# A two-layer decoder: context turned by the host's layout, first batch's parts made a stage earlier, and a fused mask and maximum

## The reference, cut to what matters

```python
x = _layernorm(x + _L0_attn_ref(x, ...))                        # 16 heads, 4 key heads, window + front
x = _layernorm(x + _L0_xattn_ref(x, ctx_2048, mask_BxS2_bk0))   # one head of width 512
x = _layernorm(x + _L0_ffn_ref(x, ...))
x = _layernorm(x + _L1_attn_ref(x, ...))                        # 16 heads of width 128, causal
x = _layernorm(x + _L1_xattn_ref(x, ctx_2048, ctx_2048))
x = _layernorm(x + _L1_ffn_ref(x, ...))

# _L0_xattn_ref
scores = jnp.einsum('bsd,bmd->bsm', hidden_states, memory_tokens) * scale
scores = jnp.where(memory_mask[:, None, :], scores, neg_inf)
attn = jax.nn.softmax(scores, axis=-1)
readout = jnp.einsum('bsm,bmd->bsd', attn, memory_tokens)
out = jnp.where(valid_b[:, None, None], readout, jnp.zeros_like(readout))
# _L1_attn_ref
scores = jnp.where(causal, scores, IGNORE); attn = softmax(scores)
```

## Time and profile before

| | |
|---|---|
| median of 3 runs | 2108.53 us (2105.29 to 2111.03) |
| profiled execution, whole | 2107.33 us |
| its span, first to last instruction | 2105.6 us |
| busy: PE, DVE, ACT, POOL | 1917.6, 1338.3, 1085.0, 638.0 us |
| mean granted clock | 0.954 |

### The profile page before, as it was taken

How to read it: one execution, slowest core, us unless ns; L and a number is a source line. 1 busy time by engine, 2 the same in 40 slices (tenths; PEclk the granted TensorE clock), 3 DMA queues, 4 the chain that set the end, 5 groups by cost and what they waited for, 6 DMA issues and landing times. The chain is left out here.

```text
span 2105.6 us, 35999 instructions
## 1 busy us (share of the span) xinstructions
PE 1917.6 (91%) x12824; PEld 1185.5 (56%) x12824; DVE 1338.3 (64%) x2579; ACT 1085.0 (52%) x2135; POOL 638.0 (30%) x558
## 2 busy tenths in 40 slices
PE   7999769989999999989999999998888876999998
PEld 4666534468887788844545454453555552455553
DVE  6777665465565755676658476687899846454333
ACT  4777543243333433356536264473799973344333
POOL 4666311123333333212101011010576740133220
PEclk9999979989999999999999999998799968999999
DMA  5000023111110111205011100003500004566433
GB/s 187 27 27 2 1 109 118 46 52 50 50 50 26 50 50 41 67 22 145 21 40 41 41 20 1 1 1 76 133 3 2 2 27 149 181 181 180 122 70 96
DMA packets 103178, 131.96 MB, mean 63 GB/s; under 512 B 8264, under 2 KB 61640, under 8 KB 103008
## 3 DMA queue, kind: packets, MB, share of 16 engines
q1 hardware_dynamic: 96304, 114.20, 17.6%
q0 software_dynamic: 6720, 15.73, 3.8%
HBM read 103.83 MB, written 22.87 MB: 60 GB/s over the span
## 5 line engine op out<-in xcount | busy, mean ns | idle before, releaser
L1113 POOL TENSOR_TENSOR wl<-stage,wh 128x512 fp32r<-128x512 f32 x80 | 116.0, 1475 | 271.9 <-DVE wh L1108 271.9
L2890 POOL TENSOR_TENSOR PTl<-P,PTh 128x512 f16<-128x512 f32 (+2 forms) x160 | 148.8, 937 | 121.1 <-ACT PTh L3014 118.4
L1699 POOL TENSOR_TENSOR Zl<-z,Zh 128x512 f16<-128x512 f32 x32 | 51.1, 1597 | 428.0 <-ACT Zh L1862 428.0
L3013 ACT ACTIVATE P<-PS 128x512 f32<-128x512 f32 (+3 forms) x256 | 143.7, 561 | 43.2 <-PE PS L2958 42.6
L77 PE MATMUL PS<-XTh,wh 128*128 128x512 f16 x416 | 159.2, 383 | 7.4 <-DVE tri L2024 5.4
L78 PE MATMUL PS<-XTl,wh 128*128 128x512 f16 x416 | 158.9, 382 | 0.0
L79 PE MATMUL PS<-XTh,wl 128*128 128x512 f16 x416 | 158.7, 381 | 0.0
L3014 ACT ACTIVATE PTh<-PS 128x512 f16<-128x512 f32 (+3 forms) x256 | 145.4, 568 | 0.0
L3030 DVE TENSOR_REDUCE M<-PS 128x1 f32<-128x640 f32 (+3 forms) x128 | 127.0, 1012 | 4.4 <-PE PS L2942 4.4
L1351 ACT ACTIVATE h<-PS,bup 128x512 f32<-128x512 f32 x64 | 44.1, 689 | 147.0 <-PE PS L79 146.3
L2958 PE MATMUL PS<-QS,KS 98*128 98x512 f16 (+3 forms) x256 | 99.6, 390 | 18.6 <-ACT PTh L3014 14.2
(11 more groups left out here) (381 smaller groups left out, 5893.5 us busy)
## 6 DMA issues: line engine op xcount, KB each, us to landing
stage<-in_ffn_W SPq DMA_DIRECT2D x18, 1024.0 KB, 5.2
stage<-in_ffn_Wg SPq DMA_DIRECT2D x9, 1024.0 KB, 5.2
stage<-in_ffn_Wup SPq DMA_DIRECT2D x16, 512.0 KB, 3.9
stage<-in_ffn_Wdn SPq DMA_DIRECT2D x16, 512.0 KB, 3.7
wq<-in_attn_wq SPq DMA_DIRECT2D x4, 1024.0 KB, 6.6
C<-in_ctx SPq DMA_DIRECT2D x8, 512.0 KB, 8.3
stage<-in_ffn_Wsw SPq DMA_DIRECT2D x16, 256.0 KB, 3.4
stage<-in_attn_WV SPq DMA_DIRECT2D x16, 256.0 KB, 4.5
```

Source lines behind the costliest of these rows:

```text
L1113: self.c.nc.gpsimd.tensor_tensor(self.piece(self.low[q], ch), self.piece(self.stage, ch), plain(self.piece(self.high[q], ch)), ALU.subtrac ...
L1699: nc.gpsimd.tensor_tensor(Zl[:, hh, to], z32[:, uu % 2, :], Zh[:, hh, to], ALU.subtract).then_inc(z_lo, 1)
L2890: ops.tensor_tensor(PTl[:, (CT * n + kt) % RING, cols], P32[:, (CT * n + kt) % SLOTS, cols], PTh[:, (CT * n + kt) % RING, cols], ALU.subtr ...
L3013: nc.scalar.activation(P32[:, i % SLOTS, cols], c.PS[:, 4 + i % 2, cols], ACT.Exp, scale=SC)
```

## The change

Three parts. (1) The host also passes the context turned (`ctxT`, a layout of the same numbers), and `turn_context` is gone. A new object `Cross0Front` holds the first batch's turned parts, two stages for pieces of 256 context rows, the mask, the mask row and the ones; its memory is that of the second cross attention's front, not yet in use. The first batch's four pieces are loaded and split during the first self-attention (units 6, 7, 14, 15), its mask row is made after unit 8; `wh` and `wl` there go from four slots to two. (2) In the first cross attention, ACT and DVE split four plain context tiles ahead of the first maximum and four in round 0, pieces 4 to 7 (the second batch) in rounds 0 and 1, and context tiles 8 to 15 in rounds 2 and 3; `Vh` holds one batch; the stores move. (3) In the second self-attention the mask product goes, and DVE's reduction and scaling become one `tensor_tensor_reduce` as in the first; PE's bank is free at that maximum; ACT's exponential reads `Pr` in place. `causal` is a new 128 x 512 constant. The bias comes first on DVE, PE waits for no constant, and DVE's four groups are all written out.

```diff
 # phase_attn1, SP
+            sp.dma_start(causal[:], c.inp["c_causal"]).then_inc(causal_in, 16)
 # PE, scores
-                need(pe, exp_done, QT * u + qt - 1)
+                need(pe, max_done, QT * u + qt - 1)
                 products(pe, out, (Qh[:, q, 0, tok], Ql[:, q, 0, tok]),
-                         (Qh[:, q, 1, 0:w], Ql[:, q, 1, 0:w]), stop=False)
-                pe.matmul(c.PS[:, 2 + qt % 2, w - P:w], c.identb[:], tri[:], start=False, stop=True,
-                          skip_group_check=True).then_inc(s_done, 1)
+                         (Qh[:, q, 1, 0:w], Ql[:, q, 1, 0:w])).then_inc(s_done, 1)
-            pe.wait_ge(const_done, 2)
             body(0)
 # ACT, exp
-                act.wait_ge(bias_done, QT * u + qt + 1)
-                need(act, t_done, QT * (u - 1) + qt + 1)
-                nc.scalar.activation(Pr[:, qt, 0:w], c.PS[:, 2 + qt % 2, 0:w], ACT.Exp, bias=nbias[:, i:i + 1],
-                                     scale=SC, accum_out=rsum[:, i:i + 1]).then_inc(exp_done, 1)
+                act.wait_ge(max_done, QT * u + qt + 1)
+                nc.scalar.activation(Pr[:, qt, 0:w], Pr[:, qt, 0:w], ACT.Exp, bias=nbias[:, i:i + 1],
+                                     scale=-1.0, accum_out=rsum[:, i:i + 1]).then_inc(exp_done, 1)
-            act.wait_ge(const_done, 3)
+            act.wait_ge(bias_ready, 1)
 # DVE, maximum
-                nc.vector.tensor_reduce(nmax[:, i:i + 1], c.PS[:, 2 + qt % 2, 0:(qt + 1) * P], AX.X, ALU.max,
-                                        negate=True).then_inc(max_done, 1)
-                dve.wait_ge(max_done, QT * u + qt + 1)
-                nc.vector.tensor_scalar(nbias[:, i:i + 1], nmax[:, i:i + 1], SC, None, ALU.mult).then_inc(bias_done, 1)
+                need(dve, t_done, QT * (u - 1) + qt + 1)
+                if isinstance(u, int) and u == 0 and qt == 2:
+                    dve.wait_ge(shifted, NT)
+                w = (qt + 1) * P
+                nc.vector.tensor_tensor_reduce(out=Pr[:, qt, 0:w], in0=c.PS[:, 2 + qt % 2, 0:w], in1=causal[:, S - w:S],
+                                               scale=-SC, scalar=FAR, op0=ALU.add, op1=ALU.min,
+                                               accum_out=nbias[:, i:i + 1]).then_inc(max_done, 1)
 # DVE, start of the stage
+            dve.wait_ge(bias_in, 16)
+            nc.vector.tensor_scalar(bq[:], bq[:], XS, None, ALU.mult).then_inc(bias_ready, 1)
             dve.wait_ge(front.const_in, 48)
             (casts of triT and tri)
+            dve.wait_ge(const_done, 2)
+            dve.wait_ge(causal_in, 16)
+            for g in range(NG):
+                body(g, g < NG - 1)

+class Cross0Front:
+    PIECES = 4
+    def load(self, sp, i):
+        b, n = divmod(i, self.PIECES)
+        need(sp, self.ct_lo, i - 1)
+        src = self.c.inp["ctxT"][b][:, n * self.W:(n + 1) * self.W].rearrange("(k p) s -> p k s", p=P)
+        sp.dma_start(self.stage[i % 2][:], src).then_inc(self.piece_in[i % 2], 16)
+    def split_hi(self, act, i):
+        act.wait_ge(self.piece_in[i % 2], 16 * (i // 2 + 1))
+        self.c.nc.scalar.activation(self.part(self.high, i), self.stage[i % 2][:], ACT.Copy, scale=XS).then_inc(self.ct_hi, 1)
+    def split_lo(self, dve, i):
+        dve.wait_ge(self.ct_hi, i + 1)
+        self.c.nc.vector.scalar_tensor_tensor(out=self.part(self.low, i), in0=self.stage[i % 2][:], scalar=XS,
+                                              in1=self.part(self.high, i), op0=ALU.mult, op1=ALU.subtract).then_inc(self.ct_lo, 1)
+    def mask_row(self, dve): ...

 # phase_attn0:  AHEAD = [U - 2, U - 1, 2 * U - 2, 2 * U - 1], U = 8
+            after.load_mask(sp)
             for g in range(1, KVH):
+                for i in (2 * g - 2, 2 * g - 1) if g < 3 else ():
+                    after.load(sp, i)
                 load(g)
+                if u in AHEAD:
+                    after.split_hi(act, AHEAD.index(u))        # ACT, end of unit u
+                if u in AHEAD:
+                    after.split_lo(dve, AHEAD.index(u))        # DVE, end of unit u
+                if u == U:
+                    after.mask_row(dve)
+                need(dve, a_done, (REP + 1) * B * (g - 1))     # DVE weights: wh[:, g % 2], wl[:, g % 2]

 # phase_cross0
+        def split_at(t):
+            pieces = [PIECES + 2 * t, PIECES + 2 * t + 1] if t < PIECES // 2 else []
+            first = CT + 4 * (t - PIECES // 2)
+            return pieces, [i for i in range(first, first + 4) if CT <= i < NC]
 # SP
+            for i in range(CT // 2):
+                load(i)
+            front.load(sp, PIECES)
+            front.load(sp, PIECES + 1)
+            for i in range(CT // 2, NC // 2):
+                load(i)
+            front.load(sp, PIECES + 2)
+            front.load(sp, PIECES + 3)
+            store_turned(0)
+            store_values(0)
+            store_turned(1)
             sp.wait_ge(c_lo, NC)
             weights.load(sp, 0, 0)
+            store_values(1)
 # PE: the calls of turn_context and the waits on its tiles go; scores wait for ct_lo, PIECES * (b + 1)
 # ACT: for t in range(4): context_high(t), then in round t
                 exponential of tile t
+                for i in range(4, CT) if t == 0 else ():
+                    context_high(i)
                 high part of the turned weights
+                for i in pieces:
+                    front.split_hi(act, i)
+                for i in tiles:
+                    context_high(i)
 # DVE: for t in range(4): context_low(t), then maximum(0), and in round t
                 maximum(t + 1)
+                for i in range(4, CT) if t == 0 else ():
+                    context_low(i)
                 ...
+                for i in pieces:
+                    front.split_lo(dve, i)
+                for i in tiles:
+                    context_low(i)
```

More of the change, by code:

```diff
@@ L1654, in phase_attn1 @@
         bq = sb("bq", [P, 3, H], F32)
-        tri = cross.tri
+        causal = sb("causal", [P, S], F32)
         Qh = sb("Qh", [P, 2, 2, S], F16)
@@ L2027, in _, with __init__, load_mask, part @@
-            body(0, True)
-            with dve.Fori(1, NG - 1) as g:
-                body(g, True)
-            body(NG - 1, False)
-            norm.late(norm.dve_step, dve)
-def phase_attn0(c, **end):
+            nc.vector.tensor_copy(cross.tri[:], front.tri32[:]).then_inc(const_done, 1)
+            dve.wait_ge(const_done, 2)
+            dve.wait_ge(causal_in, 16)
+            for g in range(NG):
+                body(g, g < NG - 1)
+            norm.late(norm.dve_step, dve)
+class Cross0Front:
+    PIECES = 4
+    W = S2 // PIECES
+    def __init__(self, c, ctx):
+        self.c = c
+        names = [("CTh", [P, KD, S2], F16), ("CTl", [P, KD, S2], F16), ("stage0", [P, KD, self.W], F32), ("stage1", [P, KD, self.W], F32),
+                 ("m32", [P, B, S2 // 4], I32), ("mrow", [1, B, S2], BF16), ("ones", [1, P], BF16)]
+        size = sum(int(np.prod(shape[1:])) * (2 if dt in (F16, BF16) else 4) for _, shape, dt in names)
+        CTh, CTl, *self.stage, self.m32, self.mrow, self.ones = Region(c, c.nc.sbuf_usable_end // 32 * 32 - size, size).place(names)
+        self.high, self.low = [CTh], [CTl]
+        sem = lambda name: ctx.enter_context(c.nc.semaphore(f"cross0_{name}"))
+        self.piece_in, self.m_in = [sem(f"piece{q}_in") for q in range(2)], sem("m_in")
+        self.ct_hi, self.ct_lo, self.m_done = sem("ct_hi"), sem("ct_lo"), sem("m_done")
+    def load(self, sp, i):
[3 more added lines that the diff above has]
+        sp.dma_start(self.stage[i % 2][:], src).then_inc(self.piece_in[i % 2], 16)
+    def load_mask(self, sp):
+        sp.dma_start(self.m32[:], self.c.inp["mask"].partition_broadcast(P)).then_inc(self.m_in, 16)
+    def part(self, parts, i):
+        b, n = divmod(i, self.PIECES)
+        return parts[b][:, :, n * self.W:(n + 1) * self.W]
+    def split_hi(self, act, i):
[5 more added lines that the diff above has]
+                                              in1=self.part(self.high, i), op0=ALU.mult, op1=ALU.subtract).then_inc(self.ct_lo, 1)
+    def mask_row(self, dve):
+        dve.wait_ge(self.m_in, 16)
+        self.c.nc.vector.tensor_scalar(self.mrow[:], self.m32[:].bitcast(U8)[0:1], 1.0, -NEG, ALU.subtract, ALU.mult).then_inc(self.m_done, 1)
+        self.c.nc.vector.memset(self.ones[:], 1.0).then_inc(self.m_done, 1)
@@ L2046, in phase_attn0 @@
+def phase_attn0(c, after, **end):
     nc = c.nc
@@ L2570, in _, with phase_cross0 @@
                 norm.low(dve, t)
-def phase_cross0(c, weights, **end):
+def phase_cross0(c, weights, front, **end):
     nc = c.nc
@@ L2584, in phase_cross0 @@
         Ch, Cl = sb("Ch", [P, NC, D], F16), sb("Cl", [P, NC, D], F16)
-        CTh, CTl = sb("CTh", [P, KD, B, S2], F16), sb("CTl", [P, KD, B, S2], F16)
-        m32 = sb("m32", [P, B, S2 // 4], I32)
-        m8 = m32[:].bitcast(U8)
+        for b in range(1, B):
+            front.high.append(sb(f"CTh{b}", [P, KD, S2], F16))
```

(28 more changed lines are left out.)

119 lines of the change are left out of this document (44 added, 75 removed).

## The result

The changed kernel took 2076.74 us (median of 4 runs, 2071.97 to 2083.16), the kernel before 2106.91 beside it (4 runs, 2102.07 to 2111.03): ratio 0.986, 95% interval 0.983 to 0.989. The forecast was 2070 with a range of 2055 to 2084. The profiled execution took 2083.16 us around a span of 2081.4, 24.2 less than the profiled 2107.33 of before.

The account below looks back on a forecast made before the run. PE, busy 91% of the span, was taken as the bound, with DVE and its chain pacing second self-attention units with a weight split. Terms -26 + 7 - 18 = -37 took 2107.33 to 2070 us; 80% range 2055 to 2084.

Parts of the forecast that it names:

- Part 1: First cross attention: context turning and mask-row wait leave PE, first turn 24.8 us earlier; -26 us, bounds -29 to -20.
- The 1 us charged for late loads: First cross attention, round 1: loads of pieces 6 and 7 may delay exponentials; 1 us, bounds 0 to 7.
- The lower bound of -29: First cross attention: best case for the sum of -24.8, -2.0 and +1, given as -29 us.
- Part 2: First self-attention: four piece splits and the mask row added there cost +7 us, bounds 2 to 15.
- The ratio of 0.69: First self-attention: 3.3 us of DVE weight-split work cost 2.27 us of span, used to price the inserts.
- the 10 us reckoned by it: First self-attention: low parts blocked by POOL cost up to 1.06 us more each, 10 us instead of 7.
- Part 3: Second self-attention: fused mask and maximum, no mask products on PE, earlier start; -18 us, bounds -25 to -9.
- in the 14 units that carry a weight split I take 0.9: Second self-attention: gain of 0.9 us per weight-split unit, between 0.22 and 1.48; 12.6 us in all.
- the 1.48 us of difference: Second self-attention: units with a weight split take 11.10 us, without 9.62; DVE and its chain set the former's pace.
- Rival (a): Second self-attention: DVE's saving does nothing, the exponential and normalisation chain holds weight units; -9, 2079 us, chance 0.18.
- The start term: Second self-attention's start: PE no longer waits for the mask's cast; 2.5 us gained.
- Rival (d): First self-attention: five inserts each drop PE's clock, a unit growing up to 6.7 us; 2111 us, chance 0.03.

Follow-up runs that it names:

- e2: The changed kernel with the old second self-attention, so only the two edits around the cross attention: 2085.49 us, ratio 0.990.
- e3: The changed kernel with DVE's low part of each piece split ahead made one unit later (units 7, 8, 15, 16): 2073.65 us, ratio 0.984.
- e10: e9 with the low part in the first self-attention moved inside its unit, behind the first maximum: 2060.79 us, ratio 0.979.
- e4: The changed kernel with the query's low part behind the maxima of tiles 2 and 3 in the second self-attention: 2076.12 us, ratio 0.985.
- e9: The changed kernel with e3, e4 and second self-attention weight parts halved, one half behind the next unit's first two normalisations: 2063.92 us, ratio 0.980.
- e5: The changed kernel with the old scaling kept on DVE behind each second self-attention maximum, waited for by nobody: 2079.98 us, ratio 0.988.
- e1: The kernel before with the new second self-attention alone (mask and maximum in one operation): 2096.57 us, ratio 0.995.
- e12: The changed kernel run again unedited, on the chip used for e10: 2075.19 us, ratio 0.985.
- e6: The changed kernel with the mask products kept on PE in the second self-attention: 2078.01 us, ratio 0.986.
- e7: The changed kernel with nothing split ahead: pieces 0 to 3 split at the cross attention's opening, 2 and 3 loaded there: 2076.33 us, ratio 0.986.

## Why the forecast was right in part 1, and where it was wrong

**Part 1** (-26, measured -26.5, -27.1 in e2). The steps held one by one: PE starts at the opening, first turn 14.3 us behind it forecast and 14.5 measured (24.8 us gone, as forecast), rounds of 12.1 us from the second turn on. The 1 us charged for late loads wasn't needed. The lower bound of -29 isn't what its terms give: -24.8 and -2.0 with no loads waited for are -26.8. Nor is -25 in part 3: all of 1.48 us in 14 units, 4.0 and 2.5 are 27.2.

**Part 2** (+7, measured +9.0 between units 0 and 30, 8.4 to 9.0 in its repeats). The ratio of 0.69 from the earlier trace rows was the wrong tool. Those inserts are DVE work with nothing to wait for. Here DVE waits for ACT, and both durations stand one behind the other: 4.05 us in units 6 and 14. Units 7 and 15, where two parts follow each other, cost 1.46 and 0.47, and the mask row 0.6, which the next unit gave back. The forecast was only near because cheap and dear inserts averaged out. The low part took 2.17 us beside POOL's operation (83.58 to 84.85) and 1.23 in unit 7, where POOL was idle: both read their inputs from SBUF, and DVE finished 1.08 us behind POOL's end. Eleven low parts of the changed kernel, e3 and e10 met that operation of POOL; they took 1.28 to 2.26 us, and all of them ended 1.07 to 1.09 us behind its end. The rule of the Trainium skill, page "SBUF — State Buffer", section "Who interferes with whom", says that the two exclude each other, and this trace agrees. That the 10 us reckoned by it are about as near to the 9 measured as my 7 is luck: only two of the four low parts were held up (2.17 and 2.16 us, the others 1.23 and 1.28), and the greater part of the cost was DVE's wait for ACT, which both sums priced at 0.69 of its length.

**Part 3** (-18, measured -10.6). The step that failed is "in the 14 units that carry a weight split I take 0.9". It was 0.37 on the average, in all kinds of unit, and nothing where one group follows another (55.20 us before, 55.21 after). I had read DVE's 36.72 of 44.38 us and the 1.48 us of difference as DVE's pace, and passed over PE's 42.64 in the same row.

Part of the 1.48 us was made by where the windows end. Both windows of the earlier trace rows run from one DVE maximum to another, and a weight part ahead of a maximum moves that end, so that the window takes in more of PE's work: it holds 260 PE instructions in four units, 65 each, and 113 in two, 56.5 each. From mark to mark of PE's own, the first score product of each unit, units 0 to 6 of the second group take, in us:

| unit | 0 | 1 | 2 | 3 | 4 | 5 | 6 |
|---|---|---|---|---|---|---|---|
| before | 10.19 | 10.13 | 10.23 | 11.39 | 10.18 | 11.32 | 10.07 |
| after | 9.81 | 9.85 | 9.82 | 10.91 | 9.79 | 10.94 | 9.76 |
| e4 | 9.63 | 9.67 | 9.70 | 10.94 | 9.71 | 10.93 | 9.59 |
| e9 | 9.63 | 9.67 | 9.59 | 9.93 | 9.59 | 9.94 | 9.59 |

Windows of units 2 and 3 before and after and of unit 3 in e9, and a row of PE's waits in the whole stage, after (us in total, times, longest):

```profile
1104.66:1114.89 10.23, 10.05 (x63) 5.59 (x63) 8.63 (x24) 7.35 (x19) 1.64 (x1) 1.00 0.01 2
1114.89:1126.28 11.39, 10.20 (x62) 5.58 (x63) 9.79 (x24) 7.51 (x19) 2.70 (x1) 1.00 0.29 95
...
1083.30:1093.12 9.82, 9.71 (x59) 5.51 (x59) 8.11 (x23) 7.29 (x19) 1.64 (x1) 1.00 0.00 0
1093.12:1104.03 10.91, 10.10 (x58) 5.37 (x59) 9.23 (x24) 7.38 (x19) 2.71 (x1) 1.00 0.29 98
...
1083.46:1093.39 9.93, 9.92 (x60) 5.46 (x59) 8.99 (x24) 7.46 (x19) 1.64 (x1) 1.00 0.30 98
...
PE PS L77 <- DVE nbias L1967: 3.3, 7, 0.5
```

So not 14 units were held but seven: those in which a weight's low part (2.28 us) stands ahead of the first maximum, two in each of three groups and one in the last. The high parts (1.22 us) cost next to nothing. The earlier trace rows had said so, with seven waits for the bank. In these seven units 1.2 us lay open, and the change took 0.4 of them, no more than off any other unit: PE's wait at the bank fell from 0.95 us to 0.46 and from 6.9 to 3.3 us in all, but didn't go, since the maximum that PE now waits for is itself queued behind the weight's low part. e4 left the seven as they were and took 0.1 to 0.2 off the others; e9, which halves the low part, took 1.0 off each of the seven, and no wait for a maximum is left among PE's.

Rival (a), with 0.18, had the nearer time, 2079, and was right that a chain holds these units. As it stood it wasn't borne out: DVE's saving did bring something (e5), and the link that holds the seven units is DVE's own weight part.

The start term was mis-sized as well. The first maximum came 10.04 us behind the opening instead of 12.74, 2.7 earlier (2.5 forecast). But the first unit then took 11.82 us instead of 10.35, so 1.2 stayed. Windows of that unit's first half, after:

```profile
936.90:942.80 5.90, 5.90 (x25) 2.68 (x24) 1.70 (x8) 2.33 (x6) 0.69 (x1) 0.71 1.09 268
```

At a granted clock of 0.71 PE was full for 5.90 us; the same stretch of before shows 1.00. After the change the clock is at its lower level twice, from about 927 to 930.5 and from about 937.3 on, behind a stop of PE of 2.60 us; before, once, from about 944 to 951, ahead of the first unit. The old code does no better at such a clock: in e2 its first unit took 12.04 us with 0.71 in its first 5.90 us. With the new code the unit took 11.81 (e1) at 0.71 and 11.51 (e12) at 0.77. So the part of the start that was lost again goes with the clock.

**Rival (d)** came true in small. Windows of the changed kernel around the first insert:

```profile
86.00:88.00 2.00, 0.31 (x2) 0.34 (x3) 1.50 (x6) 1.83 (x5) 0.06 (x1) 0.85 0.45 133
88.00:90.00 2.00, 2.00 (x10) 1.11 (x9) 1.46 (x6) 1.93 (x4) 1.55 (x2) 0.50 0.38 133
90.00:92.00 2.00, 2.00 (x11) 1.05 (x9) 1.04 (x3) 1.05 (x4) 1.92 (x2) 0.79 0.04 8
```

Behind 2.49 us without work the clock fell to the lower level (1.2 GHz) for some 3 us, and unit 7 took 8.32 us, against 7.33 in unit 15, where PE stood as long and the clock stayed at 1.00. It costs 1 us at most, not 6.7. In e3, without the stop, the same stretch shows 1.00 throughout.

Six kernels (the changed one, e2, e4, e5, e6, e12) share this code and have the stop of 2.48 or 2.49 us twice, ahead of units 7 and 15. Nine of the twelve stops were followed by a dip. The three units without one took 7.33 or 7.34 us. Those with one, by the granted clock in the unit's first 4 us: 7.32 to 7.34 at 0.86 to 0.89 (e2, e5, e6, e12), 7.74 to 7.82 at 0.80 or 0.81 (e2, e6, e12), 8.11 at 0.76 (e4), 8.32 at 0.70 (the changed kernel). So the 1 us goes with the clock, and how much of a dip is paid goes with how early in the unit it falls.

Left open: whether the shares of e5 and e6 in part 3 add up, and so how large the share of the shorter chain is; and what the last 0.3 us are by which the seven units are longer in e9, where PE shows no waits. No run separates these.

## What to carry to other kernels

Price an insert by what its engine must wait for, not by its duration: DVE's low part directly behind ACT's high part cost 4.05 us a time, and one unit of distance took 4.1 of the 9.0 us of all inserts away (e3). Where units repeat, an engine that looks nearly full may still not be the pace; take the windows from mark to mark of the engine whose pace you want, and see that they hold equal work. Follow the ring from one maximum to the next through all engines, look for the dispensable link that stands last in it, and move half of that (e9, 7.6 us beyond e4), rather than shortening what happens to be busiest. And moving work ahead into a stage that is itself full (PE 22.23 of 22.42 us) only moves the time: e7 equals the changed kernel.

## What the hardware showed that I hadn't expected

- The fused 384-wide mask and maximum reads its causal operand from SBUF and its scores from PSUM, and steps in 0.47 us (1088.67 to 1089.14), as the form in the first self-attention did; at 512 columns it lasts 0.69.
- A low clock doesn't follow each wait of the same length: of twelve stops of 2.48 or 2.49 us with the same code around them, nine brought the lower level and three left the clock at 1.00.
- A low part on DVE that met POOL's operation ended 1.07 to 1.09 us behind POOL's end, eleven times of eleven, whatever its own start. Its duration in the profile (1.28 to 2.26 us) is mostly wait.
- A half weight part (128x1024) takes 1.22 us where the whole takes 2.28, and a half high part 0.69 where the whole takes 1.22. Halving costs 0.16 us a part and still won.
